# Softmax sums stored once per head, inverted as 16 rows and spread by a product; first expert's weights rounded from main step 25; identity loaded one stage sooner

## What is computed

```python
x = L0_attn_x                       # [1, 2048, 512]
xn = _layernorm(x)
x = x + _L0_attn_ref(xn, ...) + _L0_ffn_ref(xn, ...)
# _L0_attn_ref: 16 heads of 32 features
scores = einsum('bhid,bhjd->bhij', q, k) * scale + alibi_causal_bias(s, 16)
out = einsum('bhij,bhjd->bhid', softmax(scores), v)
return out @ Wo + bo
# _L0_ffn_ref: each token goes to one of two experts (argmax of xn @ Wg.T),
# expert 0: gelu MLP, expert 1: relu MLP, 512 -> 1024 -> 512
```

## Time and profile before

| | us |
|---|---|
| median of 3 runs (lowest, highest) | 2032.83 (2027.39, 2034.80) |
| the profiled execution, its own time | 2035.95 |
| its span in the trace | 2034.1 |
| attention stage, about | 169 to 933 |
| projection stage, about | 933 to 1092 |
| experts stage, about | 1092 to 1320 |

### The profile page before, as it was taken

One profiled execution on the slowest core, in us unless ns is written; L12 is line 12 of the kernel. 1 busy time (PEld: TensorE's weight loads), 2 busy tenths in 40 slices (PEclk: granted clock), 3 DMA queues, 4 the chain that ended last, 5 costly groups with the idle time before them and its releaser, 6 DMA issues. The chain is left out here.

```text
span 2034.1 us, 22765 instructions
## 1 busy us (share of the span) xinstructions
PE 1698.3 (83%) x8338; PEld 1103.0 (54%) x8338; DVE 981.8 (48%) x1582; ACT 586.3 (29%) x806; POOL 645.3 (32%) x527
## 2 busy tenths in 40 slices
PE   6996499999999999994445999923999996499997
PEld 5883244444444444442334777712776774378886
DVE  7654356656666666633544555544334435022222
ACT  3120054434444444452111221223233232022221
POOL 4000357588687680001113666612001001000000
PEclk9996589989999999997767999955999998789999
DMA  7758234453446443003432112165102201612210
GB/s 238 245 186 185 29 94 116 91 148 100 92 131 144 99 121 68 11 17 119 150 129 84 58 58 63 55 219 202 42 1 84 83 1 42 227 68 83 82 41 21
DMA packets 108804, 204.71 MB, mean 101 GB/s; under 512 B 27914, under 2 KB 42010, under 8 KB 106826
## 3 DMA queue, kind: packets, MB, share of 16 engines
q1 hardware_dynamic: 80830, 131.72, 22.4%
q0 software_dynamic: 13648, 51.61, 8.5%
q10 hardware_dynamic: 14224, 20.02, 2.9%
HBM read 134.10 MB, written 68.96 MB: 100 GB/s over the span
## 5 line engine op out<-in xcount | busy, mean ns | idle before, releaser
L924 DVE TENSOR_REDUCE att_maxes<-att_unit 128x1 f32<-128x512 f32 (+3 forms) x640 | 386.0, 611 | 290.9 <-PE att_unit L794 177.7
L906 ACT ACTIVATE att_probs<-att_scores 128x1024 f32<-128x1024 f32 (+1 forms) x320 | 285.5, 895 | 373.2 <-PE att_scores L823 187.5
L840 PE MATMUL att_outp<-att_probs,att_vs 128*64 128x512 f32 (+3 forms) x1280 | 308.8, 562 | 0.0
L794 PE MATMUL att_unit<-moew_wbh,moew_wah 100*128 100x512 f32 (+2 forms) x320 | 152.3, 492 | 9.4 <-DMA moew_wbh<-alibi_k_rounded 4.9
L1509 PE MATMUL glu_u<-glu_xh,glu_w 128*128 128x512 f32 x352 | 138.9, 395 | 18.9 <-DMA glu_xl<-zn_lo 18.9
L794 PE MATMUL att_unit<-moew_wbl,moew_wal 100*128 100x512 f32 (+2 forms) x320 | 138.3, 439 | 0.6
L1510 PE MATMUL glu_u<-glu_xl,glu_w 128*128 128x512 f32 x352 | 138.4, 393 | 0.0
L823 PE MATMUL att_scores<-moew_wah,moew_wbh 102*128 102x512 f32 (+2 forms) x320 | 110.2, 417 | 28.4 <-ACT att_probs L906 28.4
L794 PEld LDWEIGHTS att_unit<-moew_wbh,moew_wah 100*128 100x128 f32 x320 | 67.2, 212 | 121.5 <-DVE att_maxes L924 80.7
L794 PEld LDWEIGHTS att_unit<-moew_wbl,moew_wal 100*128 100x128 f32 x320 | 60.2, 190 | 117.0 <-DVE att_maxes L924 81.7
L267 PE MATMUL proj_acc<-moew_woh,proj_ath 128*128 128x512 f32 x64 | 32.9, 513 | 97.4 <-DVE proj_atl L1097 97.4
(11 more groups left out here) (274 smaller groups left out, 3543.9 us busy)
## 6 DMA issues: line engine op xcount, KB each, us to landing
att_q_raw<-in_w POOLq DMA_DIRECT2D x48, 352.0 KB, 3.9
w_ternary<-att_q_out POOLq DMA_DIRECT2D x24, 352.0 KB, 2.6
glu_w<-w_ternary ACTq DMA_DIRECT2D x9, 768.0 KB, 11.7
xn<-qkv_x SPq DMA_DIRECT2D x4, 1024.0 KB, 6.7
q_hi<-qkv_hi SPq DMA_DIRECT2D x16, 256.0 KB, 3.2
q_lo<-qkv_lo SPq DMA_DIRECT2D x16, 256.0 KB, 3.7
k_hi<-qkv_hi SPq DMA_DIRECT2D x16, 256.0 KB, 2.6
k_lo<-qkv_lo SPq DMA_DIRECT2D x16, 256.0 KB, 3.3
```

Source lines behind the costliest of these rows:

```text
L794: last = pe.matmul(unit[:, h, 0:cover], qs[par][0:SROWS, h, t * P:(t + 1) * P], ks[par][0:SROWS, h, g * CH:g * CH + cover], start=True, st ...
L840: last = pe.matmul(outp[v_cols(h), c % 2, off:CH], vs[p % 2][:, kt, v_cols(h)], probs[:, g % 4, h, off:CH], start=kt == 0, stop=kt == TT * ...
L906: act.activation(probs[:, g % 4, :, off:CH], scores[:, g % 2, :, off:CH], ACT.Exp).then_inc(exped, 1)
L924: dve.tensor_reduce(maxes[:, h, t, g:g + 1], unit[:, h, 0:width], AX.X, ALU.max).then_inc(unit_taken, 1)
```

## The change

1. In attention SP stores one row of each head's sums, not 32; the tensor `softmax_sums` has 16 rows, not 512.
2. ACT makes the hi parts of `ahead` at main steps 25, 27, ... 55, not 1, 3, ... 31.
3. In projection the tiles `su` and the eight reciprocals of 128 x 1024 are gone. DVE clears a tile `inv` of 128 x 512, SP loads the 16 rows of sums into it for each of 4 chunks (at partitions 0, 32, 64, 96), DVE inverts it once. For each half PE spreads the 16 rows over 128 x 4 x 256 in PSUM (`wide`, two buffers) with a 0/1 matrix `spread`, loaded by ACT; DVE multiplies `at` by `wide`.
4. SP loads `at` of half `n + 2` as soon as the lo part of half `n` is made, ahead of the wait for the additions.
5. `ident` is a tile of the surrounding scope, loaded by SP in projection; `experts_stage` has no tile, load and wait of its own for it.

```diff
         LOADS = 4
+        SPLIT_FROM = 25
@@ attention, sync
-                    sp.dma_start(sum_d[(p * 2 + h) * HD:(p * 2 + h + 1) * HD, c * CH:(c + 1) * CH],
-                                 att[s:s + HD, c % 2, :]).then_inc(stored[c % 2], 16)
+                    sp.dma_start(sum_d[p * 2 + h:p * 2 + h + 1, c * CH:(c + 1) * CH], att[s:s + 1, c % 2, :]
+                                 ).then_inc(stored[c % 2], 16)
@@ attention, scalar
-                if g % 2 and g // 2 < len(ahead):
-                    ws.hi(act, g // 2)
+                if g >= SPLIT_FROM and g % 2 and (g - SPLIT_FROM) // 2 < len(ahead):
+                    ws.hi(act, (g - SPLIT_FROM) // 2)
@@ projection, sync
+            sp.wait_ge(cleared, 1)
+            for c in range(NCH):
+                sp.dma_start(inv[c * QUAD:c * QUAD + NH, :], sum_d[:, c * CH:(c + 1) * CH]).then_inc(sum_in, 16)
+            load_att(0)
+            load_att(1)
+            load_rows(0)
+            load_rows(1)
+            sp.dma_start(ident[:], cst_d[:, 0, :]).then_inc(ident_in, 16)
             for n in range(NHC):
+                if n + 2 < NHC:
+                    load_att(n + 2)
                 sp.wait_ge(added, (n + 1) * PER)
                 sp.dma_start(half_rows(out_d, n), y_half(n)).then_inc(stored[n % 2], 16)
                 if n + 2 < NHC:
-                    load(n + 2)
+                    load_rows(n + 2)
@@ projection, tensor
+            def widen(n):
+                c, s = n // 2, slice(n % 2 * HC, (n % 2 + 1) * HC)
+                heads = slice(c * QUAD, c * QUAD + NH)
+                if n >= 2:
+                    pe.wait_ge(scaled, n - 1)
+                for k in range(KT):
+                    last = pe.matmul(wide[n % 2][:, k, :], spread[heads, k, :], inv[heads, s], start=True, stop=True)
+                last.then_inc(widened, 1)
+            pe.wait_ge(spread_in, 16)
+            pe.wait_ge(inverted, 1)
+            widen(0)
+            widen(1)
             for n in range(NHC):
...
+                if n + 2 < NHC:
+                    widen(n + 2)
@@ projection, vector
-                dve.reciprocal(su[n % 2][:], su[n % 2][:]).then_inc(inverted, 1)
-                dve.wait_ge(inverted, n + 1)
-                dve.tensor_tensor(at[n % 2][:], at[n % 2][:], su[n % 2][:], ALU.mult).then_inc(scaled, 1)
+                dve.wait_ge(widened, n + 1)
+                dve.tensor_tensor(at[n % 2][:], at[n % 2][:], wide[n % 2][:], ALU.mult).then_inc(scaled, 1)
...
+            dve.memset(inv[:], 1.0).then_inc(cleared, 1)
             dve.tensor_scalar(rt.take[:], rt.idx[:], float(T - 1), None, ALU.min).then_inc(clamped, 1)
+            dve.wait_ge(sum_in, NCH * 16)
+            dve.reciprocal(inv[:], inv[:]).then_inc(inverted, 1)
```

More of the change, by code:

```diff
@@ L1011, in gather, with projection_stage @@
     return pool.indirect_dma_start(out, None, rows_d, bass.IndirectOffsetOnAxis(ap=rt.take[:, j:j + 1], axis=0))
-def projection_stage(nc, w, rt, xg, xn_d, x_d, att_d, sum_d, out_d):
+def projection_stage(nc, w, rt, xg, ident, spread_d, cst_d, xn_d, x_d, att_d, sum_d, out_d):
     HC = CH // 2
     NHC, PER = T // HC, HC // P
+    QUAD = P // NCH
     with Stage(nc, "proj") as st:
-        at, su = ([st.sb(f"{n}{i}", [P, KT, HC]) for i in range(2)] for n in ("at", "su"))
+        at = [st.sb(f"at{i}", [P, KT, HC]) for i in range(2)]
         ath, atl = ([st.sb(f"{n}{i}", [P, KT, HC], F32R) for i in range(2)] for n in ("ath", "atl"))
+        inv, spread = st.sb("inv", [P, CH]), st.sb("spread", [P, KT, P])
         y = st.sb("y", [P, 4, D])
         acc = st.ps("acc", [P, 4, D])
+        wide = [st.ps(f"wide{i}", [P, KT, HC]) for i in range(2)]
         ws = WeightSplit(st, FH, w.second, 3)
         at_in, x_in = ([st.sem(f"{n}{i}") for i in range(2)] for n in ("at_in", "x_in"))
-        inverted, scaled = st.sem("inverted"), st.sem("scaled")
+        cleared, sum_in, spread_in, ident_in = st.sem("cleared"), st.sem("sum_in"), st.sem("spread_in"), st.sem("ident_in")
+        inverted, widened, scaled = st.sem("inverted"), st.sem("widened"), st.sem("scaled")
         hi_ready, lo_ready = st.sem("hi_ready"), st.sem("lo_ready")
@@ L1039, in _, with load_att, load_rows @@
         def _(sp):
-            def load(n):
+            def load_att(n):
                 if n >= 2:
                     sp.wait_ge(lo_ready, n - 1)
-                for dst, src in ((at, att_d), (su, sum_d)):
-                    sp.dma_start(dst[n % 2][:], feat(src)[:, :, n * HC:(n + 1) * HC]).then_inc(at_in[n % 2], 16)
+                sp.dma_start(at[n % 2][:], feat(att_d)[:, :, n * HC:(n + 1) * HC]).then_inc(at_in[n % 2], 16)
+            def load_rows(n):
                 if n >= 2:
@@ L1071, in _ @@
                     last.then_inc(made, 1)
+                if n + 2 < NHC:
+                    widen(n + 2)
         @block.scalar
         def _(act):
+            act.dma_start(spread[:], spread_d).then_inc(spread_in, 16)
             for j in range(3):
@@ L1118, in _, with spread_heads, experts_stage @@
             pool.wait_ge(gathered, 2 * 16)
-def experts_stage(nc, w, rt, xg, cst_d, ba_d, bb_d, bo_d, xn_d, x1a_d, x1_d):
+def spread_heads():
+    row, k, m = np.arange(P)[:, None, None] % 32, np.arange(KT)[None, :, None], np.arange(P)[None, None, :]
+    return (row == k * HPG + m // HD).astype(np.float32)
+def experts_stage(nc, w, rt, xg, ident, ba_d, bb_d, bo_d, xn_d, x1a_d, x1_d):
     HT = FT // 2
     with Stage(nc, "moe") as st:
-        ident = st.sb("ident", [P, P])
         ba, bb, bo = st.sb("ba", [P, 2, FH]), st.sb("bb", [P, 2, D]), st.sb("bo", [P, D])
@@ L1135, in experts_stage @@
         up, down = st.ps("up", [P, 2, CH]), st.ps("down", [P, 2, D])
[L1136 removed]
+        b_in, b_ready = st.sem("b_in"), st.sem("b_ready")
         gathered, fetched, stored = ([st.sem(f"{n}{i}") for i in range(k)]
@@ L2044, in build @@
                 xg = [xst.sb(f"xg{n}", [P, D]) for n in range(2)]
-                projection_stage(nc, w, rt, xg, xn_d, i["x"], att_d, sum_d, x1a_d)
-                experts_stage(nc, w, rt, xg, i["att_cst"], i["ba"], i["bb"], i["bo"], xn_d, x1a_d, x1_d)
+                ident = xst.sb("ident", [P, P])
+                projection_stage(nc, w, rt, xg, ident, i["spread_heads"], i["att_cst"], xn_d, i["x"], att_d, sum_d, x1a_d)
+                experts_stage(nc, w, rt, xg, ident, i["ba"], i["bb"], i["bo"], xn_d, x1a_d, x1_d)
     with Stage(nc, "linw") as st:
```

11 lines of the change are left out of this document (4 added, 7 removed).

## The result

The changed kernel took 1935.62 us (median of 4 runs, 1930.83 to 1938.06) against 2030.54 for the kernel before (2027.39 to 2034.80): a ratio of 0.953, with a 95% interval of 0.950 to 0.956. Run again beside other kernels (`e_again`) it took 1928.83, median of five from 1926.19 to 1941.73, ratio 0.950 (0.947 to 0.952). 1921 had been forecast, 1909 to 1938 as the range: the time lies in the range, 14.6 us over the forecast.

The account below looks back on a forecast made before the run. PE was taken to bound attention; in projection no engine was full, a ring of dependent steps set the time. Savings of 31.9 + 80.2 + 0.4 = 112.5 us from 2035.95 gave 1923.4, for the median 1921, range 1909 to 1938.

Parts of the forecast that it names:

- The stall, 28.4: Attention, step 2: with weight pieces from step 25 on, nothing stands before the exponentials, which removes PE's wait of 28.4 us.
- The clock, 3.5: Attention, steps 4 to 8: without the stall PE's clock stays up, saving 4 x 0.87 = 3.5 us.
- The moved work: nothing.: Attention from step 25: ACT's idle time holds the moved pieces; cost nothing, at most 1 us for each of four large pieces.
- The quantizer 21 us later: covered.: POOL in attention: its quantizer begins 21 us later, covered by the 174.38 us POOL was idle after it.
- Projection's start, 15.5: Start of projection: from the stage's begin near 933.5, PE starts the first half at 949.0 in place of 954.52.
- The pace, 7.5: Projection: each half takes 7.5 us, with PE needing 7.3 and SP's ring 6.9.
- (a): Rival, projection: transfers set the pace, at 8.7 us a half the time is 1929; chance 0.15.
- (b): Rival, projection: PE's clock falls in each half; 1933 (chance 0.10), or 1966 at half clock throughout (chance 0.03).
- (c): Rival, attention steps 2 to 24: ACT or PE waits for POOL elsewhere, 32 us stay, time 1953; chance 0.04.
- (d): Rival, attention from step 2: the low clock lasts long; over 0.5% slower than before after 437 us of it; chance 0.02.
- Its own signs: Wrong if projection's starts are over 9 us apart, PEclk there under 0.8, or a new wait in attention's first 55 steps.
- The sum: Whole kernel: 31.9 (attention) + 80.2 (projection) + 0.4 (identity) = 112.5 us saved.

Follow-up runs that it names:

- e_reduces: The changed kernel with the reduce, cast and subtraction that close a head's maxes on DVE replaced by four reduces: 1920.80 us, ratio 0.945.
- e_sums_first: The changed kernel with ACT's weight loads in projection waiting for the sums, and the reciprocal in two halves: 1927.72 us, ratio 0.949.
- e_late_load: The changed kernel with the next load of `at` in projection issued behind the store of a half, as before the change: 1955.11 us.
- e_split_1: The changed kernel with the weight pieces from main step 1 again: 1952.50 us, ratio 0.962.
- e_split_only: The kernel before with only the late start of the weight pieces, from main step 25: 2008.95 us, ratio 0.989.
- e_quiet_pool: The changed kernel without POOL's quantizing arithmetic, its loads and stores kept, so the last layer gets other weights: 1925.88 us.

## Why the prediction was right, and where it was not

- **The stall, 28.4.** Right. The exponentials of step 4 went from 257.56 to 228.87, 28.7 sooner.
- **The clock, 3.5.** In the changed kernel's trace this term was 0.8: step 8 came 29.45 sooner, since PE stayed at half clock to 237. `e_again` did the same. In the traces of `e_reduces`, `e_sums_first` and `e_late_load`, with the same work in these steps, the clock rose at 224 to 226 and step 8 began at 235 to 236 in place of 240; there the term was 4.3. It is there in some executions and not in others; as a fixed gain it was mis-sized.
- **"The moved work: nothing."** This step failed. It looked at ACT's room between exponentials, and not at two other things that a moved piece meets. One is its load, which at step 47 came beside SP's loads of a head pair: 5.4 us of the gain went between steps 46 and 48 (25.9 to 20.5). The other is POOL's lo part, which near step 29 held DVE's cast and took 2.2 us (29.44 at step 24, 27.25 at step 32). The kernel before lost 4.9 us more than the changed one between steps 83 and 88, in the same way, after a cast of 1.80 us beside the quantizer, so the two traces end 26.4 apart. That the trace before has this loss is luck of this pair of traces.
- **The quantizer 21 us later: covered.** It began 30.0 us later and POOL was idle for 114.8 us behind it. Right as an idle time, wrong as a thing without effect: which casts it holds changes with its place, and this makes one execution differ from another.
- **Projection's start, 15.5.** It was 19.4. Nearly all of it is the sums' landing, 8.4 for an estimate of 5.0 (4.6 with ACT's loads held back). It left out that ACT's weight loads start at the same time. The rest of the chain was as said: reciprocal 3.35 for 3.3, the first four spreading products 3.9 with the handing over for 3.6, and 3.6 to the first of `proj_acc`. The four of the second half stood ahead of it too, but ended at 925.92, before the lo part; they cost nothing. The slow start of the first half took 1.9 us for 1.4.
- **The pace, 7.5.** 7.60, with PE as the bound and PEclk at 1.00: 5.7 for the 24 products and 1.9 for the four spreading ones. The forecast had 7.3 for PE and 0.2 for the transfers; the size was right, and its reason for the last 0.2 was not. Rivals (a) and (b) did not come; `e_late_load` shows that the margin was thin, since one later load brings the pauses and the falling clock every second half, and 10.6 us. What the Trainium skill says in "TensorE: Matmul & The Clock Gate", section "HAM oscillation — how this bites in real kernels", that waits for data between short groups of products make PE restart slow each time, fits that run (a first product of 0.79 to 0.80 us after each of the three pauses) and not the changed kernel, where PE has no such waits.
- **Rivals (c) and (d).** `e_split_1` rules out (c): the wait belongs to the pieces' place. Half clock for hundreds of us, (d), was in no run.
- **Its own signs.** One that it had named for being wrong did come: a new wait in attention's first 55 steps, ACT's 6.7 us and PE's 3.1 at step 47. PEclk was not at 0.9 from 230 on either but from 238, and the stage took 83 us for 78. The other two stayed away: starts 7.60 apart, PEclk 1.00 from 930 to 982. The total held because the lost terms are small beside the stall and the pace.
- **The sum.** 112.5 against 105.1 between the two executions: 5.5 short in attention, 4.7 in projection, 2.6 more in the rest (luck, as said above), and 0.2 outside the spans. That is 7.4 of the 14.6 us by which the median missed (1930.83 for 1923.4). The other 7.2 are the base: 2.4 had been taken off because the profiled execution before was slow for its kernel, and the one after was 4.8 under its own median.

## What to carry to other kernels

When work is moved to a "free" stretch, ask what each engine's share of it meets there: its loads beside other loads, and GpSimd's elementwise work beside VectorE's casts and two-input instructions. Where TensorE is the bound, a pause of 1.4 to 2.2 us can cost 2 to 10 us by the half clock behind it, as it did in most of these traces. So small VectorE instructions on SBUF tiles that TensorE waits for are best written as reduces, and small loads that start a stage are best issued alone.

## What the runs showed of the hardware

A cast of 128 x 8 on VectorE took 0.17 us, and up to 2.54 beside GpSimd's 2.05 us instruction (`e_late_load`; 2.47 in `e_again`); the subtraction with two inputs took up to 2.27 (`e_split_only`). Reduces of the same size stayed at 0.17 to 0.19, 128 of them in `e_reduces`, 73 of which ran beside GpSimd's work. Not every cast is held: the one of 16 x 128 that reads PSUM took 0.27 to 0.28 in all 32 chunks of every trace, though 21 of the 32 ran beside GpSimd's work in the changed kernel. The Trainium skill has this rule in "SBUF — State Buffer", section "Who interferes with whom": casts that run in a two-port mode, and instructions with two SBUF inputs, contend with GpSimd for a shared port pair, which one of them holds for its whole instruction, and reduces never do on this chip. The runs agree on casts, two-input instructions and reduces. Who of the two came first they don't show: the cast of 612.54 is read as 0.39 us ahead of the instruction that it ended with. The runs add the price behind it: after waits of 1.4 to 2.2 us PE's granted clock often went from 1.00 to 0.50, the lower of its two levels, and stayed there for 3 to 17 us though PE was busy. It did not always: in `e_quiet_pool` a wait of 1.61 us and in `e_reduces` one of 2.42 brought no fall.

At the start of attention PE was busy in every stretch from 221 to 237 and still had half clock in two executions of the changed kernel, while in the nine other traces with moved pieces it rose between 224 and 230, two of them (`e_sums_first`, `e_late_load`) with the same attention program. What decides this stays open.
